# Test-time memory on one core: the chunk loop written out, the query products moved behind the state update, norms computed with fewer instructions

## What is computed

```
g = _grad_fn(W_state, k[:, sl], v[:, sl]) * GRAD_SCALE        # 0.1; loss = sum((silu(k @ W1.T) @ W2.T - v) ** 2)
gn = jnp.maximum(jnp.linalg.norm(g, axis=-1, keepdims=True), EPS)
g = g * jnp.minimum(MAX_GRAD_NORM / gn, 1.0)
# for each token: S = eta * S - theta * g;  W = (1 - alpha) * W + S
h = jax.nn.silu(jnp.einsum('btd,btod->bto', q[:, sl], W1t))
outs.append(jnp.einsum('bto,btpo->btp', h, W2t))
```

## Time and profile before

| | us |
|---|---|
| three runs | 4681.85, 4685.8, 4686.91 |
| median | 4685.8 |
| profiled execution, its own time | 4681.54 |
| profiled execution, span from first to last instruction | 4679.7 |

### The profile page before, as it was taken

The page is one execution under the profiler, slowest core; times in us unless marked ns, Lnnn a source line. Parts: engine busy times, 40 slices in busy tenths (PEclk is TensorE's granted clock), DMA queues, the critical chain, the costliest instruction groups (busy, mean ns, idle before and its releaser), DMA issues.

```text
span 4679.7 us, 114797 instructions
## 1 busy us (share of the span) xinstructions
PE 3977.7 (85%) x46878; PEld 2233.9 (48%) x46974; DVE 3228.5 (69%) x5280; ACT 2529.5 (54%) x3698; POOL 1193.6 (26%) x1015
## 2 busy tenths in 40 slices
PE   3688888888888888866668999999998499999997
PEld 1355555555555555534434555555554133333333
DVE  7688878888888788854432665656664577667772
ACT  4356666666666565652122555555553266666665
POOL 0255556555556555500000000000000011111110
PEclk7899999999999999965567999999999699999999
DMA  0122222222222222200000000000000301110000
GB/s 17 65 59 77 62 61 73 67 58 78 61 71 65 60 81 61 60 15 17 19 13 16 3 2 4 4 4 3 4 1 6 114 2 24 21 26 17 19 2 14
DMA packets 84462, 166.49 MB, mean 36 GB/s; under 512 B 22472, under 2 KB 36472, under 8 KB 82704
## 3 DMA queue, kind: packets, MB, share of 16 engines
q1 hardware_dynamic: 83952, 159.13, 13.0%
HBM read 40.60 MB, written 8.52 MB: 10 GB/s over the span
## 4 chain that ended last, share of the span: by engine, by line
PE 63%; DVE 13%; issue 11%; ACT 8%; DMA 2%; SPq 2%; POOL 1%; DVEq 0%; POOLq 0%; ACTq 0%
PE banks L503 6%; PE banks L1238 5%; PE banks L2178 5%; PE banks L1209 4%; PE banks L1221 4%; PE banks L582 4%; PE banks L598 3%; PE banks L544 3%; PE banks L618 2%; PE banks L561 2%; ACT arena L2316 2%; PE banks L2152 2%; PE banks L535 2%; ACT arena L710 2%; PE banks L2136 2%
## 5 line engine op out<-in xcount | busy, mean ns | idle before, releaser
L2390 DVE TENSOR_REDUCE arena<-banks 128x2 f32<-128x1024 f32 x512 | 614.0, 1222 | 277.9 <-PE banks L2143 141.8
L2316 ACT ACTIVATE arena<-banks 128x1024 f32<-128x1024 f32 x512 | 522.8, 1025 | 282.7 <-PE banks L2159 147.2
L939 POOL TENSOR_TENSOR arena<-arena 128x512 f32<-128x512 f32 x384 | 425.4, 1129 | 755.1 <-DVE arena L824 747.5
L943 POOL TENSOR_TENSOR arena<-arena 128x1024 f32<-128x1024 f32 x192 | 533.0, 2776 | 15.1
L1391 DVE CUSTOM_DVE_ANT_0 arena<-arena,banks 128x512 f32<-128x512 f32 (+3 forms) x640 | 361.6, 602 | 235.2 <-issue 233.9
L1334 ACT ACTIVATE arena<-banks 128x512 f32<-128x512 f32 (+3 forms) x320 | 170.1, 532 | 418.9 <-PE banks L1221 418.2
L503 PE MATMUL banks<-arena 128*128 128x512 f32 x768 | 355.6, 607 | 31.4 <-ACT arena L673 24.4
L2178 PE MATMUL banks<-arena 128*32 128x256 f32 x4096 | 334.5, 393 | 17.2 <-issue 11.6
L1326 ACT ACTIVATE arena<-arena 128x128 f32<-128x128 f32 (+15 forms) x256 | 328.5, 1285 | 11.2 <-DVE arena L1403 6.3
L1209 PE MATMUL banks<-arena 64*128 64x512 f32 (+3 forms) x1280 | 326.1, 582 | 9.2 <-issue 8.0
L1221 PEld LDWEIGHTS banks<-consts,arena 128*128 128x128 f32 x2176 | 233.1, 141 | 189.6 <-DVE arena L1410 102.4
(11 more groups left out here) (432 smaller groups left out, 7618.2 us busy)
## 6 DMA issues: line engine op xcount, KB each, us to landing
arena<-arena SPq DMA_DIRECT2D x768, 64.0 KB
arena<-arena SPq DMA_DIRECT2D x96, 384.0 KB, 3.6
arena<-arena SPq DMA_DIRECT2D x96, 128.0 KB, 3.4
arena<-in_lf_wqkv SPq DMA_DIRECT2D x6, 1024.0 KB, 5.3
arena<-features_k SPq DMA_DIRECT2D x32, 128.0 KB
arena<-arena SPq DMA_DIRECT2D x8, 512.0 KB
arena<-features_q SPq DMA_DIRECT2D x16, 216.0 KB
arena<-in_lf_wqkv SPq DMA_DIRECT2D x6, 512.0 KB, 3.8
```

What stands on the lines that cost most here:

```text
L939: nc.gpsimd.tensor_tensor(r[:, :, e * H2:(e + 1) * H2], q[:, j, :, (1 - e) * H2:(2 - e) * H2], s[:, j, 1, e * H2:(e + 1) * H2].unsqueeze(1 ...
L943: nc.gpsimd.tensor_tensor(a, a, lf_rb, ALU.add).then_inc(S("lf_rot" + x), 1)
L2316: nc.scalar.activation(bi_PT[n % 4], PS[:, 2 * bi_slot("S", n):2 * bi_slot("S", n) + 2].rearrange("p a b -> p (a b)"), ACT.Exp).then_inc(S ...
L2390: nc.vector.tensor_reduce(bi_max[j % 2][:, t, :, c], PS[:, 2 * slot:2 * slot + 2], AX.X, ALU.max).then_inc(S("bi_mx"), 1)
```

## The change

- `tt_rounds` writes all 32 rounds out; waits are against constants. SP's loop is written out too.
- PE: ret part 0 of chunk n moves from behind z of round n + 1 to the end of round n, behind the update products. Ret part 1 moves up, between z and the prediction. L1693 takes 32 columns as its stationary side in place of 128.
- ACT: the sigmoid of the query rows comes ahead of z's. The squares of h start as soon as h is there, those of dp after dp, each into its own half of `tt_sq`. The product of the two sums is now an ACT operation (Identity with one sum as its scale), with 1e-10 added as the floor.
- DVE: L1888 and L1903 go. The silu of the query rows (L1931) comes first in the round, L1934 ahead of dp, L1936 behind it. L1897 and L1899 become one operation. The limit is 0.1 in place of 1, and the factor 0.01 is gone: the table of coefficients is ten times as large (-0.1/32 in the mask).
- POOL waits for the squared norm directly.
- New semaphores `tt_hab` (L1934 done) and `tt_zc` (copy L1892 done); `tt_u` waits for the latter.

```diff
@@ -1581,7 +1581,7 @@
...
 tt_zp = arena.f32(2 * MD)
-tt_sq = arena.f32(MD)
+tt_sq = arena.f32_3(2, MD)
 tt_n = arena.f32(8)
...
@@ -1628,22 +1628,18 @@
...
         sp.dma_start(tt_r[n][tok], tt_rp[tok, n]).then_inc(S(f"tt_r_in{n}"), 16)
-    with sp.Fori(1, NM // 2) as i:
-        for p in range(2):
-            sp.wait_ge(S("tt_state"), i * 2 + (p - 1))
-            sp.dma_start(tt_g[p][tok], tt_gp[tok, bass.ds(i * 2 + p, 1)].rearrange("p o f -> p (o f)")).then_inc(S(f"tt_g_in{p}"), 16)
-            sp.wait_ge(S("tt_rout"), i * 2 + (p - 1))
-            sp.dma_start(tt_r[p][tok], tt_rp[tok, bass.ds(i * 2 + p, 1)].rearrange("p o f -> p (o f)")).then_inc(S(f"tt_r_in{p}"), 16)
+    for n in range(2, NM):
+        sp.wait_ge(S("tt_state"), n - 1)
+        sp.dma_start(tt_g[n % 2][tok], tt_gp[tok, n]).then_inc(S(f"tt_g_in{n % 2}"), 16)
+        sp.wait_ge(S("tt_rout"), n - 1)
+        sp.dma_start(tt_r[n % 2][tok], tt_rp[tok, n]).then_inc(S(f"tt_r_in{n % 2}"), 16)
...
-    grad(0, 0, 0, None)
-    with eng.Fori(0, NM // 2 - 1) as i:
-        grad(i * 2 + 1, 1, i, lambda j: ret(i * 2, 0, i, j))
-        grad(i * 2 + 2, 0, i + 1, lambda j: ret(i * 2 + 1, 1, i, j))
-    last = NM // 2 - 1
-    grad(NM - 1, 1, last, lambda j: ret(NM - 2, 0, last, j))
+    for n in range(NM):
+        grad(n, n % 2, n // 2, (lambda j: ret(n - 1, (n - 1) % 2, (n - 1) // 2, j)) if n else None)
...
@@ -1678,43 +1674,43 @@
...
         if ret:
-            ret(0)
+            ret(1)
         pe.wait_ge(S("tt_h"), n + 1)
...
         nc.tensor.matmul(PS[tok, 1, 64:96], tt_h[p][lo, 0:64], s[lo, 96:128], start=True, stop=True).then_inc(S("tt_pred"), 1)
-        if ret:
-            ret(1)
         pe.wait_ge(S("tt_dp"), n + 1)
...
         u = tt_u[tok, 0:2]
-        nc.tensor.matmul(PS[:, 3, 0:64], g[tok, G_kt:G_kt + P], u[:, :, 0:32], start=True, stop=True)
+        nc.tensor.matmul(PS[lo, 3, 0:64], g[tok, G_kt:G_kt + 32], u[:, :, 0:32], start=True, stop=True)
         nc.tensor.matmul(PS[lo, 3, 64:128], tt_h[p][tok, 64:96], u[:, :, 32:64], start=True, stop=True)
...
         nc.tensor.matmul(PS[lo, 3, 160:192], u[:, 1, 32:64], tt_h[p][tok, 64:96], start=True, stop=True).then_inc(S("tt_upd"), 1)
+        r = tt_r[p]
+        pe.wait_ge(S(f"tt_r_in{p}"), pair * 16 + 16)
+        pe.wait_ge(S("tt_rsteps"), n + 1)
+        nc.tensor.matmul(PS[tok, 4, 0:64], s[lo, 32:96], r[lo, R_q:R_q + 64], start=True, stop=False, skip_group_check=True)
+        nc.tensor.matmul(PS[lo, 4, 0:64], s[lo, 0:32], r[lo, R_q + 64:R_q + 128], start=False, stop=False, skip_group_check=True)
+        nc.tensor.matmul(PS[lo, 4, 0:64], tt_rs[p][tok, 0:32], r[tok, R_m:R_m + 64], start=False, stop=True, skip_group_check=True).then_inc(S("tt_rz"), 1)
     def ret(n, p, pair, j):
-        s, r = tt_st[p], tt_r[p]
-        if j == 0:
-            pe.wait_ge(S(f"tt_r_in{p}"), pair * 16 + 16)
-            pe.wait_ge(S("tt_rsteps"), n + 1)
-            nc.tensor.matmul(PS[tok, 4, 0:64], s[lo, 32:96], r[lo, R_q:R_q + 64], start=True, stop=False, skip_group_check=True)
-            nc.tensor.matmul(PS[lo, 4, 0:64], s[lo, 0:32], r[lo, R_q + 64:R_q + 128], start=False, stop=False, skip_group_check=True)
-            nc.tensor.matmul(PS[lo, 4, 0:64], tt_rs[p][tok, 0:32], r[tok, R_m:R_m + 64], start=False, stop=True, skip_group_check=True).then_inc(S("tt_rz"), 1)
+        s = tt_st[p]
         if j == 1:
...
         if j == 2:
+            pe.wait_ge(S("tt_hab"), n + 1)
             pe.wait_ge(S("tt_rm"), n + 1)
-            pe.wait_ge(S("tt_ret"), n + 0)
+            if n:
+                pe.wait_ge(S("tt_ret"), n)
             nc.tensor.matmul(PS[tok, 6, 0:64], s[lo, 96:160], tt_hab[lo, 0], start=True, stop=False, skip_group_check=True)
...
     tt_rounds(pe, grad, ret)
-    for j in range(3):
+    for j in (1, 2):
         ret(NM - 1, 1, NM // 2 - 1, j)
...
@@ -1777,17 +1773,19 @@
...
     def grad(n, p, pair, ret):
+        if ret:
+            ret(0)
         act.wait_ge(S("tt_z"), n + 1)
         nc.scalar.activation(tt_sg[p][tok], PS[tok, 0, 0:96], ACT.Sigmoid).then_inc(S("tt_sg"), 1)
+        act.wait_ge(S("tt_h"), n + 1)
+        nc.scalar.activation(tt_sq[tok, 0], tt_h[p][tok, 64:96], ACT.Square, accum_out=tt_n[tok, 0:1]).then_inc(S("tt_sqs"), 1)
+        act.wait_ge(S("tt_dp"), n + 1)
+        nc.scalar.activation(tt_sq[tok, 1], tt_dp[tok, 64:96], ACT.Square, accum_out=tt_n[tok, 1:2]).then_inc(S("tt_sqs"), 1)
+        act.wait_ge(S("tt_sqs"), n * 2 + 2)
         if ret:
-            ret(0)
-        act.wait_ge(S("tt_dp"), n + 1)
-        if ret:
-            act.wait_ge(S("tt_n2"), n + 0)
-            act.wait_ge(S("tt_sqs"), n * 2)
-        nc.scalar.activation(tt_sq[tok], tt_h[p][tok, 64:96], ACT.Square, accum_out=tt_n[tok, 0:1]).then_inc(S("tt_sqs"), 1)
-        act.wait_ge(S("tt_sqs"), n * 2 + 1)
-        nc.scalar.activation(tt_sq[tok], tt_dp[tok, 64:96], ACT.Square, accum_out=tt_n[tok, 1:2]).then_inc(S("tt_sqs"), 1)
+            act.wait_ge(S("tt_n2"), n)
+        nc.scalar.activation(tt_n[tok, 2:3], tt_n[tok, 1:2], ACT.Identity, scale=tt_n[tok, 0:1], bias=1e-10).then_inc(S("tt_n01"), 1)
         if ret:
...
@@ -1797,9 +1795,7 @@
...
             act.wait_ge(S("tt_rout"), n + 1)
-            at = n * MC
-            dst = tt_ret[lo, at:at + MC] if isinstance(n, int) else tt_ret[lo, bass.ds(at, MC)]
-            nc.scalar.activation(dst, PS[lo, 6, 0:64], ACT.Copy).then_inc(S("tt_ret"), 1)
+            nc.scalar.activation(tt_ret[lo, n * MC:(n + 1) * MC], PS[lo, 6, 0:64], ACT.Copy).then_inc(S("tt_ret"), 1)
...
@@ -1878,46 +1876,40 @@
...
         if ret:
-            ret(0)
+            ret(1)
         dve.wait_ge(S(f"tt_g_in{p}"), pair * 16 + 16)
...
         if ret:
-            ret(1)
-        dve.wait_ge(S("tt_sqs"), n * 2 + 2)
-        nc.vector.tensor_tensor(tt_n[tok, 2:3], tt_n[tok, 0:1], tt_n[tok, 1:2], ALU.mult).then_inc(S("tt_n01"), 1)
+            ret(2)
         dve.wait_ge(S("tt_dp"), n + 1)
         if ret:
-            dve.wait_ge(S("tt_u"), n + 0)
-        nc.vector.tensor_copy(tt_zp[tok, 32:64], tt_dp[tok, 64:96])
+            dve.wait_ge(S("tt_rsteps"), n)
+        nc.vector.tensor_copy(tt_zp[tok, 32:64], tt_dp[tok, 64:96]).then_inc(S("tt_zc"), 1)
         dve.wait_ge(S("tt_dh"), n + 1)
...
         dve.wait_ge(S("tt_dz"), n + 1)
-        nc.vector.tensor_tensor(tt_t1[tok], tt_zp[tok, 0:32], tt_zp[tok, 0:32], ALU.mult).then_inc(S("tt_dz2"), 1)
-        dve.wait_ge(S("tt_dz2"), n + 1)
-        nc.vector.tensor_reduce(tt_n[tok, 3:4], tt_t1[tok], AX.X, ALU.add).then_inc(S("tt_dzn"), 1)
+        nc.vector.tensor_tensor_reduce(tt_t1[tok], tt_zp[tok, 0:32], tt_zp[tok, 0:32], 1.0, 0.0, ALU.mult, ALU.add, tt_n[tok, 3:4]).then_inc(S("tt_dzn"), 1)
         dve.wait_ge(S("tt_dzn"), n + 1)
+        dve.wait_ge(S("tt_n01"), n + 1)
         nc.vector.scalar_tensor_tensor(out=tt_n[tok, 4:5], in0=tt_n[tok, 3:4], scalar=g[tok, G_k2:G_k2 + 1], in1=tt_n[tok, 2:3], op0=ALU.mult, op1=ALU.add).then_inc(S("tt_n2"), 1)
-        dve.wait_ge(S("tt_n2"), n + 1)
-        nc.vector.tensor_scalar(tt_n[tok, 5:6], tt_n[tok, 4:5], 0.01, 1e-12, ALU.mult, ALU.max).then_inc(S("tt_gn2"), 1)
         dve.wait_ge(S("tt_clip"), n + 1)
-        nc.vector.scalar_tensor_tensor(out=tt_ec[tok], in0=tt_n[tok, 6:7].broadcast_to([MC, 3]), scalar=1.0, in1=g[tok, G_ec:G_ec + 3], op0=ALU.min, op1=ALU.mult).then_inc(S("tt_ec"), 1)
+        nc.vector.scalar_tensor_tensor(out=tt_ec[tok], in0=tt_n[tok, 6:7].broadcast_to([MC, 3]), scalar=0.1, in1=g[tok, G_ec:G_ec + 3], op0=ALU.min, op1=ALU.mult).then_inc(S("tt_ec"), 1)
         dve.wait_ge(S("tt_ec"), n + 1)
+        dve.wait_ge(S("tt_zc"), n + 1)
         if ret:
-            dve.wait_ge(S("tt_upd"), n + 0)
+            dve.wait_ge(S("tt_upd"), n)
         nc.vector.tensor_tensor(tt_u[tok, 0:2], tt_zp[tok].unsqueeze(1).broadcast_to([MC, 2, 64]), tt_ec[tok, 0:2].unsqueeze(2).broadcast_to([MC, 2, 64]), ALU.mult).then_inc(S("tt_u"), 1)
         nc.vector.tensor_scalar(tt_rs[p][tok], tt_zp[tok], tt_ec[tok, 2:3], None, ALU.mult).then_inc(S("tt_rsteps"), 1)
-        if ret:
-            ret(2)
...
         if ret:
-            dve.wait_ge(S("tt_rout"), n + 0)
-            dve.wait_ge(S("tt_state"), n + 0)
+            dve.wait_ge(S("tt_rout"), n)
+            dve.wait_ge(S("tt_state"), n)
         nc.vector.scalar_tensor_tensor(out=wn, in0=old[:, :, 1], scalar=g[lo, G_s + 1:G_s + 2], in1=upd[:, :, 1], op0=ALU.mult, op1=ALU.add).then_inc(S("tt_wn"), 1)
...
@@ -1931,12 +1923,13 @@
...
             dve.wait_ge(S("tt_rh"), n + 1)
-            nc.vector.tensor_tensor(tt_hab[lo], tt_hq[lo].unsqueeze(1).broadcast_to([MD, 2, MC]), r[lo, R_ab:R_ab + 128].rearrange("p (a b) -> p a b", a=2), ALU.mult)
+            nc.vector.tensor_tensor(tt_hab[lo], tt_hq[lo].unsqueeze(1).broadcast_to([MD, 2, MC]), r[lo, R_ab:R_ab + 128].rearrange("p (a b) -> p a b", a=2), ALU.mult).then_inc(S("tt_hab"), 1)
+        if j == 2:
             dve.wait_ge(S("tt_rkh"), n + 1)
...
```

(14 more changed lines are left out.)

## The result

| | before | after |
|---|---|---|
| median of four runs | 4684.9 | 4630.65 |
| lowest and highest | 4681.85 to 4686.91 | 4623.82 to 4631.24 |
| profiled execution, its own time | 4681.54 | 4631.24 |
| its span | 4679.7 | 4629.2 |
| stage, from the first z to the first result projection | 255.8 | 209.5 |

All times in us. The ratio is 0.9881 with a 95% interval of 0.9864 to 0.9899: 54 us faster by the medians, 50.3 by the two profiled executions. The forecast was 4641 with a range of 4627 to 4657. Of the 50.5 us by which the span shrank, 46.3 lie in the stage of the change and 4.2 outside it.

A forecast was written before the change was run, and what follows sets the result against it. A chain of dependences bounds the 32 rounds: ten steps sum to 6.56 us against 7.906, 1.35 less, times 31 is 41.9, plus 1.2 for the first round, 43.1 in total. Forecast 4641 us, range 4627 to 4657.

The forecast's parts named there:

- Items 1 and 2: Query products moved behind the update: z to prediction 1.25 us instead of 1.52, last update product to next z 1.32 instead of 1.23.
- cover for L1708: Query product moved between z and the prediction is clear by 1.0 us, before the prediction at 1.25: cost 0.
- Item 3: Norm product leaves DVE's queue, so dz waits only for its own product: 0.77 us in place of 1.26.
- item 7: Loop written out: waits against registers go, mostly off the chain; 0 us (bounds 0 to 0.1 saved).
- Item 4: Square and sum of dz in one DVE operation: 0.22 us in place of 0.43 (bounds 0.18 and 0.32).
- the rule against fusing: The Trainium skill's advice on chained DVE operations: square and sum stay 0.43 us, forecast 6.5 us higher.
- Item 5: Floor operation L1903 goes: norm to POOL 0.34 us in place of 0.55 (bounds 0.30 and 0.40).
- Item 6: First update product on 32 columns: 0.25 us to the second in place of 0.61 (bounds 0.21 and 0.35).
- rival C: Packets of the written-out code come late on PE and DVE, kernel slower: 4732 us at 8.3 each; chance 0.03.
- A: PE's granted clock rises to 2.4 GHz, small products shorten: 0.6 us a round, 18 us, giving 4622; chance 0.07.
- B: Half the gain lost in queues or to code packets: 4664 us, chance 0.10; weaker forms 4651 to 4656, chance 0.05.
- D: Unseen chain link, z stays behind it: about 4660 us, chance 0.05; with a late L1708 4683, chance 0.02.

The follow-up runs named there:

- e1: Kernel before with only the chunk loop and SP's loop written out; 0.9982 of before, mean round 7.846 us.
- e3: Changed kernel with the three query products and what hangs on them back in their old order; 0.9884 of before, round 6.622 us.
- e6: Changed kernel with the product of the two sums on DVE again, ahead of the copy, without the 1e-10; 4640.1 us, most steps 6.52.
- e9: Changed kernel with both squares behind dp again, the product of the sums still on ACT; 4618.52 us, steps of 6.51.
- e5: Changed kernel with square and sum of dz as two operations again; 0.9906 of before, round 6.665 us.
- e4: Changed kernel with the first update product on 128 columns again; 0.9907 of before, round 6.85 us.
- e2: Changed kernel with the hardware loop kept from round 3 and the first update product on 128 columns; 0.9908 of before, round 6.894 us.
- e11: Changed kernel with two query products ahead of the update and gradients multiplied by coefficients while POOL works; 0.9869 of before, round 6.323 us.

## Why the prediction was right

**The bound and the items.** The chain was the right one, and the sum followed it: 6.56 forecast, 6.45 measured. Against e1, the old round written out, the steps add up without a rest: 0.17 for the query products, 0.41 to dz, 0.21 for square and sum, 0.18 for the floor and 0.40 for the update product make 1.37, and 7.82 - 6.45 is 1.37.

- Items 1 and 2, the move of the query products: 0.18 net in the forecast, 0.17 by e3. The cover for L1708 held: it starts 0.68 after z and the prediction is not late. The price of 0.09 for PE's queue is 0.08.
- Item 3: 0.49 forecast, 0.50 measured, of which 0.08 belongs to item 7, as e1 has it without any other edit. And its heading, "norm product off DVE", names only one of two sufficient causes (e6, e9). The two edits overlap for the most part, and the thin cover that I gave the product on ACT is needed only because it was moved.
- Item 4: 0.21 forecast, 0.213 by e5. The row of 128 columns, scaled down, was exact; the rule against fusing would have missed by 6.9 us.
- Item 5: from the norm to POOL 0.34 forecast, 0.29 measured. Mis-sized by 0.05: the 0.55 that I started from had the register work of the loop in it. It is 0.47 in every second round before and in all of e1's.
- Item 6: 0.36 forecast, 0.40 by e4. Mis-sized by 0.03: the first of the update products is followed after 0.22, like the second (0.21), idle stretch ahead of it or not.
- Item 7: 0 forecast. e1 shows 0.09 a round by itself, 1.9 us in the stage; on the shorter chain of the changed kernel, e2 against e4, it is 0.04. A term put at nothing, which cost the sum little, because the new steps of the other items were mostly taken free of it.

So the stage gave 46.3 us where 43.1 were forecast, the difference in terms of 0.01 to 0.05 a round each.

**The missing term.** By the profiled executions 7.2 us separate the sum of 4638.4 from 4631.24: 3.2 lie in the stage, the rest outside. The median, 10.4 below the 4641, stayed inside the range because the range was wide enough, not because a term stood for it. That the change moves all later code, and that a jump in another stage costs more or less by where it lies and by what the clock does behind it, stood in none of the items. It stood in rival C, with the wrong sign and in the wrong place: I priced late packets in the written-out code only.

**The rivals.** A is refuted: the grant stayed at 0.50 with PE at 0.77. B and C are refuted too, but not for a lack of packets: I counted 11, and the stage of the changed kernel has 17 on the two instruction queues, where it had 2 before. DMA queues over the stage of the changed kernel:

```profile
q8 instruction: 8, 0.13, 0.3%
q14 instruction: 9, 0.07, 0.1%
```

None of them stops a round there, and where rounds are stopped (e1, e3, e6, e11) it is for 0.37 us at most and not 2.1. D is refuted by the table of steps.

## What to carry to other kernels

In a chain of small dependent operations, add start-to-start steps taken from the trace; a round of ten steps came out within 2%. Ask of every instruction in a queue whether it waits for more than those behind it need, and if two edits would cure the same wait, count the cure once. When code grows or shrinks, read the jumps of hardware loops in other stages too, with the granted clock behind each, and try a few dozen idle instructions ahead of a loop before the kernel is called finished.

## What was not expected of the hardware

- A jump back in a hardware loop with a long body stopped PE for 1.55 to 2.02 us in every trace. In the kernel before a second stop of 1.82 to 2.37 us followed one product later, and 64 waits ahead of the code took it away.
- Behind such stops the granted clock fell from 1.00 to 0.50 for some us in every pass of 128.8 us and more: 16 records took 2.95 us in place of 1.74. In all a pass is 1.7 to 8.1 us over 125.4. In the chunk loop, with its short body, a jump costs 0.07 (e2).
- Straight-line code brought 17 packets of instructions into the stage, and no round of the changed kernel is longer for it; in e1, e3, e6 and e11 it cost up to 0.37 us at one to four points in 31 rounds.
- A power of one column on POOL takes 0.54 us, and 0.60 with a DVE operation of 192 columns beside it (e11).
- An Identity of one column on ACT whose scale is read from memory takes 0.295 us.
